# GpSimd zeroing of masked exponentials in twelve attention units, in place of mask products on TensorE

## The chip, the cores and the metric

The kernel runs on one core of a Trainium2 chip. The metric is the device time of one execution in microseconds. The kernel before was timed in three runs.

## What is computed

One decoder layer on 8 batches of 256 tokens, 256 features, in float32. It has three parts, each followed by a residual sum and a layer norm: self attention with 16 heads of 16 features, causal and with a window of 64 keys; cross attention to a context, 16 heads, causal, with ReLU on q, k and v; and a mixture of 8 experts, top 2, with capacity 160 in each of 2 groups. Cut to what matters here:

```python
# self attention
scores = einsum('bhid,bhjd->bhij', q, k) / sqrt(HD)
mask = (j <= i) & (j >= i - (W - 1))                 # W = 64
probs = softmax(where(mask, scores, -inf))
y = einsum('bhij,bhjd->bhid', probs, v) @ Wo.T + bo
# cross attention
scores = einsum('bqhd,bkhd->bhqk', relu(q), relu(k)) / sqrt(D)
probs = softmax(where(tril(ones), scores, NEG))
out = layer_norm(einsum('bhqk,bkhd->bqhd', probs, relu(v)) + q) * gamma + beta
# experts
dispatch, combine = top-2 routing with cumulative positions
y = combine . (relu((dispatch . x) @ wi) @ wo)
```

## The kernel before, in words

The attention work is cut into 16 units, `UNITS` (8 self "s", one for each batch, and 8 cross "c"). Units 0 to 3 are self, then they alternate: 4 is cross, 5 self, 6 cross, 7 self, 8 cross, 9 self, 10 cross, 11 self, and 12 to 15 are cross. Each unit has 12 jobs (`JOBS`), three for each of its four groups of four heads.

Each unit computes its scores twice on TensorE. The handler `N` computes them with queries on the partitions into one of two PSUM banks `nat`; VectorE takes the row maxima from them (`negm`). The maxima, split into three bf16 parts, are transposed (`MT`) and put as three extra rows under the queries. The handler `T_` then computes the transposed scores, keys on the partitions, minus these maxima, into one of two banks `byk`. ScalarE takes the exponential of a bank into `probs` (handler `T_` on ScalarE, line 769), which has two buffers, one for even and one for odd groups. Jobs 0 and 1 of a group hold the first 128 keys of two heads each, with 192 queries (self) or 256 (cross); job 2 holds the last 128 keys and queries of four heads. The handler `PV` (line 596) multiplies the exponentials by the values: 16 matmuls for a group. Ones beside the values give the sums of the softmax.

The mask comes in by TensorE: `bank_scores` starts a bank with a bf16 product of the identity and a mask tile that holds 0 and -3e38 (line 528), and then adds the score products of each head (line 532). A `byk` bank thus takes one mask product and two or four score products. The mask product is 384 columns wide for jobs 0 and 1 of a self unit, 256 for these of a cross unit, and 512 for job 2 of both.

The order of every engine's instructions is written out by hand. `in_order()` gives each piece of work a slot (a number of jobs since the start), sorts all pieces by slot into one list, `PLAN`, and each engine walks that list (`walk`) and issues the pieces it has a handler for, in that order, with blocking waits on semaphores. Unit k starts at `first_slot(k)`, 12k, plus 2 from unit 4 on; call it n0. Its `N` jobs have the slots n0 to n0+11, its `T` jobs n0+18 to n0+29 (a little earlier in units 0 to 2, by `SOONER`), its four `PV` n0+22.2+3g. ScalarE's exponential of a `T` job stands in the list at the slot of that job.

The pieces that GpSimd issues in the attention part are: `CK`, for a cross unit k at its n0-18, which splits the keys into bf16 parts. It waits for ScalarE's evacuations of that unit's key projection (`KC`, TensorE, at n0-19; ScalarE writes `parts_k` and then `fk`), and it is three operations of 128x512 (lines 1212 to 1214). `XB` (line 1221) and `XA` (line 1227), each one addition of 128x512. `VC` (line 1232), a ReLU in place on the values of a cross unit, at n0+10, which waits for VectorE's evacuation. `GS` (lines 1205 and 1252), the 16 indirect DMAs that send the tokens of the first group to the experts, from slot 166.1 on, 0.75 slots apart; some of them wait for the gates of the router or for earlier ones to land. And `ES`, the indirect DMAs of the expert outputs.

TensorE's `T_` job waits until the exponential of the job before the last has been read out of the bank; `PV` waits for the exponential of the third job of its group. The slots of `T` and `N` jobs around a `PV` run on while the exponential is computed.

After the attention the 16 expert passes run (`XT`, `H0`, `H1`, `H2`, `EY`, lines 655, 670, 684, 687), and then the last norm.

Of the kernel before, what the change touches and what calls it, by code (L numbers as in the profile page):

```python
# [8 lines left out]
ALU = mybir.AluOpType  # L9
# [3 lines left out]
P = 128  # L13
# [47 lines left out]

SOONER = {0: 6.05, 1: 4, 2: 2}
ROWS_BY_ACT = 3


CLOSING = {
# [23 lines left out]
def in_order():  # L90
# [7 lines left out]
    for k, (layer, b) in enumerate(UNITS):  # L98
        n0 = first_slot(k)
        sooner = SOONER.get(k, 0)  # L100
        if layer == "s":
            for later, earlier in X_BEFORE.items():
                if earlier == b:
                    add(n0 + (14.6 if b == 0 else 9.6), "LX", UNIT_OF["s", later])
            if b == 3:
                add(n0 + 9.7, "LC", UNIT_OF["c", 2])
            add(n0 + (14 if b == 0 else 8), "XL", k)
            for at, name in ((-12.4, "QS"), (-12.35, "SQ"), (-12.3, "KS"), (-12.2, "SK")) if b == 2 else ((-19, "QS"), (-18, "SQ"), (-17.5, "KS"), (-16.5, "SK")):
                add(n0 + at, name, k)
            for at, name in ((11.85 if b == 0 else 8.5, "VS"), (20, "XB"), (34 - sooner, "Y2"), (35 - sooner, "WO"), (36 - sooner, "R3"), (36.8 - sooner, "L3")):  # L110
                add(n0 + at, name, k)
        else:
            if b + TOK < B:
                add(n0 + 11.1, "LC", UNIT_OF["c", b + TOK])
            late = 2 if b == B - 1 else 0
            for at, name in ((-19, "KC"), (-18, "CK"), (late - 11.5, "XC"), (late - 10.2, "QC"), (late - 9.2, "SC"), (late - 6, "XA"), (10, "VC")):
                add(n0 + at, name, k)
            for at, name in CLOSING.get(k, ((n0 + 33.3, "FQ"), (n0 + 34.4, "R1"), (n0 + 35.2, "L1"), (n0 + 37, "R2"), (n0 + 37.7, "L2"),
                                            (n0 + 39.4, "XS"), (n0 + 39.5, "XR"), (n0 + 40.9, "RT"))):
                add(at, name, k)  # L120
        for j in range(JOBS):
            add(n0 + j, "N", k, j)
            add(t_slot(k, j), "T", k, j)
        add(n0 + (11.3 if k == 0 else 12), "MP", k)
        add(n0 + {0: 11.5, 1: 12.6, 2: 13.2}.get(k, 14) if k < last else 195.6, "MT", k)
        for g in range(G):
            add(n0 + 22.2 - sooner + 3 * g if k < last - 1 else t_slot(k, 3 * g + 2) + (1.1 if g < G - 1 else 0.5), "PV", k, g)
        add(n0 + 32.6 - sooner if k < last - 1 else (198.6, 206.9)[k - last + 1], "YA", k)
        add(n0 + 32.9 - sooner if k < last - 1 else (198.7, 207.0)[k - last + 1], "YB", k)
    for i, (at, _) in enumerate(LOADS):  # L130
# [58 lines left out]
def attention_and_experts(nc: bass.Bass, a, out):  # L189
    with ExitStack() as ctx:  # L190
# [124 lines left out]
        work_full = sems("work_full", WB); work_free = sems("work_free", WB)  # L315
        nat_full = sems("nat_full", 2); nat_free = sems("nat_free", 2)
        byk_full = sems("byk_full", 2); exp_ready = sem("exp_ready")
        pv_full = sem("pv_full"); yT_ready = sem("yT_ready")
        part0 = {side: sem(f"part0_{side}") for side in "qk"}
        split = {side: sem(f"split_{side}") for side in "qk"}  # L320
        stacked = {side: sems(f"stacked_{side}", PAIRS) for side in "qk"}
# [142 lines left out]
        def _(pe):  # L464
# [60 lines left out]
            def bank_scores(bank, mask, heads, w, at, emit_pair):  # L525
# [6 lines left out]
                    last = nc.tensor.matmul(bank[:, i * w:(i + 1) * w], lhsT, rhs, start=False, stop=(i == heads - 1), skip_group_check=True)  # L532
                return last

            def N(k, j, layer, b):
                q, ks = stack["q", k % PAIRS], stack["k", k % PAIRS]
                if j == 0:
                    if k == 0:
                        pe.wait_ge(masks_ready, 1)
                    pe.wait_ge(stacked["q"][k % PAIRS], SIDE * (k // PAIRS + 1))  # L540
                    pe.wait_ge(stacked["k"][k % PAIRS], SIDE * (k // PAIRS + 1))
                job = JOBS * k + j
                wait(pe, nat_free[job % 2], job // 2)
                g, i = divmod(j, 3)
                bank = nat[job % 2]
                if i == 0:
                    h0 = 4 * g
                    last = bank_scores(bank, mq0[layer], 4, P, 0, lambda h: (q[0:KR, h0 + h, 0:P], ks[0:KR, h0 + h, 0:P]))
                else:
                    h0, w = 4 * g + 2 * (i - 1), KEYS0[layer]  # L550
                    last = bank_scores(bank, mq1[layer], 2, w, w - mq1[layer].shape[2],
                                       lambda h: (q[0:KR, h0 + h, P:T], ks[0:KR, h0 + h, T - w:T]))
                last.then_inc(nat_full[job % 2], 1)
# [11 lines left out]
            def T_(k, j, layer, b):  # L565
                q, ks = stack["q", k % PAIRS], stack["k", k % PAIRS]
                if j == 0:
                    pe.wait_ge(m_rows[k % 2], 16 * MR * (k // 2 + 1))
                    if k < PAIRS:
                        pe.wait_ge(ones_in[k], 16)  # L570
                job = JOBS * k + j
                wait(pe, exp_ready, job - 1)
                g, i = divmod(j, 3)
                bank = byk[job % 2]
                if i < 2:
                    h0, w = 4 * g + 2 * i, KEYS0[layer]
                    last = bank_scores(bank, mk0[layer], 2, w, 0, lambda h: (ks[0:KR + MR, h0 + h, 0:P], q[0:KR + MR, h0 + h, 0:w]))
                else:
                    h0 = 4 * g
                    last = bank_scores(bank, mk1[layer], 4, P, 0, lambda h: (ks[0:KR + MR, h0 + h, P:T], q[0:KR + MR, h0 + h, P:T]))  # L580
                last.then_inc(byk_full[job % 2], 1)

            def PV(k, g, layer, b):
                pe.wait_ge(exp_ready, JOBS * k + 3 * g + 3)
                if g == 0:
                    if layer == "s":
                        emptied(pe, "VS", k)
                    else:
                        pe.wait_ge(v_ready, b + 1)
                if g % 2 == 0:  # L590
                    wait(pe, yT_ready, (G * k + g) // 2)
                o = (g % 2) * T
                for kt in range(QT):
                    for j in range(4):
                        cols, src = ((0, KEYS0[layer]), (0, KEYS0[layer])) if kt == 0 else ((P, T), (256, 384))
                        last = nc.tensor.matmul(pv[32 * j:32 * j + 32, o + cols[0]:o + cols[1]], vone[layer][:, b % 2, kt, 4 * g + j, :],  # L596
                                                probs[:, g % 2, j, src[0]:src[1]], start=(kt == 0), stop=(kt == QT - 1),
                                                skip_group_check=True)
                last.then_inc(pv_full, 1)
# [549 lines left out]
        def _(pool):  # L1149
# [53 lines left out]
            def put_gates(tile, tiles, k):  # L1203

                g_.tensor_copy(xres[:, tile:tile + tiles, GATE], gates[:, tile:tile + tiles, k]).then_inc(ids_ready, 1)

            def CK(k, n, layer, b):
                pool.wait_ge(part0["k"], k + 1)
                emptied(pool, "KC", k)
# [56 lines left out]
                                        out_offset=bass.IndirectOffsetOnAxis(ap=target[:, x % 2, 1:2], axis=0),  # L1266
                                        in_=ye[x % 2][:, 1, 0:ZW], in_offset=None, compute_op=ALU.add).then_inc(y_stored[x % 2], 16)

            walk({"CK": CK, "XB": XB, "XA": XA, "VC": VC, "GS": GS, "ES": ES})


def by_partition(a):
# [50 lines left out]
```

## Time and profile before

| | |
|---|---|
| median of 3 runs | 625.91 us (622.70 to 629.24) |
| the profiled execution, own time | 624.59 us |
| its span in the trace | 622.8 us |
| PE busy | 520.7 us, 84% of the span, 5092 matmuls |
| DVE busy | 338.3 us, 54% |
| ACT busy | 218.9 us, 35% |
| POOL busy | 146.8 us, 24%, 160 instructions |
| mean granted TensorE clock | 0.941 |

PE is TensorE's matmuls, PEld its weight loads, DVE VectorE, ACT ScalarE, POOL GpSimd. Busy times are of one profiled execution; 1.8 us of its own time lie outside the span. Matmuls are pipelined and their ends are modelled, so what a matmul costs is read from the distance of one start to the next. The attention part takes the span up to about 450 us, the experts follow to about 600 us.

### The profile page before, as it was taken

What the parts mean: (1) busy time and instruction counts of PE and PEld (TensorE: products, weight loads), DVE (VectorE), ACT (ScalarE), POOL (GpSimd) and SP (SyncE); (2) the same over time, 40 slices, a digit from 0 to 9 for tenths busy, and PEclk for the clock granted to TensorE, in tenths of its full rate; (3) what the DMA queues carried; (4) which work ended last, traced back from release to release, by engine and by line L of the source; (5) the groups of instructions that cost most, each with busy time, mean ns of one, the idle gap of its engine ahead of it and who ended that gap; (6) DMA issues with size and microseconds to landing.
All of it is one profiled execution on the core that took longest, in us unless ns stands there. A gap on an engine that the chain in (4) does not pass through costs nothing. (4 is left out here: it accounts for less than half of the span.)

```text
span 622.8 us, 12856 instructions
## 1 busy us (share of the span) xinstructions
PE 520.7 (84%) x5092; PEld 404.9 (65%) x5092; DVE 338.3 (54%) x952; ACT 218.9 (35%) x491; POOL 146.8 (24%) x160
## 2 busy tenths in 40 slices
PE   5179487959989989989999879799798999999960
PEld 4047265737666667767767656477587888888850
DVE  3547343746677877877677967684263202232114
ACT  2004125234445544544554625453521111232103
POOL 4000003002103004004104166000123755132330
PEclk9669779989999999999999989799999999999995
DMA  2999935693595585585449556345666634888214
GB/s 87 118 145 140 161 62 87 116 106 43 78 136 97 76 132 99 85 120 101 96 54 157 79 109 189 52 162 196 224 233 228 202 52 76 247 300 244 23 20 137
DMA packets 58840, 78.97 MB, mean 127 GB/s; under 512 B 9454, under 2 KB 52077, under 8 KB 55708
## 3 DMA queue, kind: packets, MB, share of 16 engines
q1 hardware_dynamic: 42236, 39.57, 41.1%
q10 hardware_dynamic: 10400, 33.29, 16.9%
q0 software_dynamic: 6144, 5.29, 5.3%
q8 instruction: 40, 0.66, 0.5%
q14 instruction: 20, 0.16, 0.1%
HBM read 40.32 MB, written 13.74 MB: 87 GB/s over the span
## 5 line engine op out<-in xcount | busy, mean ns | idle before, releaser
L956 DVE TENSOR_REDUCE negm<-nat 128x4 f32<-128x512 f32 (+2 forms) x192 | 120.0, 641 | 88.7 <-PE nat L532 86.5
L769 ACT ACTIVATE probs<-byk 128x512 f32<-128x512 f32 (+1 forms) x192 | 105.8, 562 | 116.0 <-PE byk L532 114.3
L532 PE MATMUL nat<-arena 96*128 96x128 bf16 (+2 forms) x512 | 73.8, 248 | 0.0
L532 PE MATMUL byk<-arena 99*128 99x128 bf16 (+2 forms) x512 | 71.8, 242 | 0.0
L532 PEld LDWEIGHTS nat<-arena 96*128 96x128 bf16 x512 | 46.9, 102 | 16.3 <-issue 3.2
L532 PEld LDWEIGHTS byk<-arena 99*128 99x128 bf16 x512 | 45.7, 99 | 18.1 <-issue 1.1
L1212 POOL TENSOR_TENSOR resk<-fk,parts_k 128x512 f32<-128x512 f32 x8 | 9.3, 1158 | 182.3 <-ACT fk L708 125.8
L528 PE MATMUL nat<-window_q,identb 128*128 128x384 bf16 (+1 forms) x96 | 35.9, 374 | 18.8 <-DMA arena<-parts_k 13.7
L528 PE MATMUL byk<-window_k,identb 128*128 128x384 bf16 (+1 forms) x96 | 34.2, 356 | 18.1 <-DMA arena<-mT 17.7
L670 PE MATMUL work<-yn_T,arena 128*128 128x160 f32 x256 | 40.1, 305 | 2.4 <-DVE r_s L1123 2.4
L670 PE MATMUL work<-woT,arena 128*128 128x160 f32 x256 | 39.8, 304 | 0.0
L528 PE MATMUL nat<-causal_q,identb 128*128 128x256 bf16 (+1 forms) x96 | 30.3, 315 | 10.2 <-DVE negm L956 5.6
L670 PEld LDWEIGHTS work<-yn_T,arena 128*128 128x128 f32 x256 | 35.6, 190 | 3.4 <-DVE r_s L1123 2.6
L478 PE MATMUL work<-xT,ws 128*128 128x256 f32 x112 | 30.9, 433 | 6.9 <-DMA xT<-in_x_T 6.9
L670 PEld LDWEIGHTS work<-woT,arena 128*128 128x128 f32 x256 | 35.5, 190 | 0.9
L1252 POOL DMA_INDIRECT expert_x<-xres,put x32 | 31.9, 995 | 12.6 <-issue 7.8
L528 PE MATMUL byk<-causal_k,identb 128*128 128x256 bf16 (+1 forms) x96 | 30.2, 315 | 0.8 <-ACT probs L769 0.7
L478 PEld LDWEIGHTS work<-xT,ws 128*128 128x128 f32 x112 | 23.9, 220 | 10.9 <-issue 5.8
L684 PE MATMUL work<-arena,ws 128*128 128x256 f32 x128 | 29.1, 380 | 0.7 <-ACT ws L859 0.7
L1221 POOL TENSOR_TENSOR xres<-xres,rows 128x512 f32<-128x512 f32 x8 | 10.2, 1269 | 82.1 <-DMA xres<-in_x 82.1
L684 PE MATMUL work<-arena,xT 128*128 128x256 f32 x128 | 29.1, 380 | 0.0
L596 PE MATMUL pv<-probs,v_c 128*32 128x128 f32 (+1 forms) x512 | 28.1, 338 | 0.7 <-ACT probs L769 0.7
(189 smaller groups left out, 895.3 us busy)
## 6 DMA issues: line engine op xcount, KB each, us to landing
arena<-parts_q SPq DMA_DIRECT2D x96, 128.0 KB, 5.1
arena<-parts_k SPq DMA_DIRECT2D x96, 128.0 KB, 5.4
arena<-in_ffn_wi ACTq DMA_DIRECT2D x12, 1024.0 KB, 5.5
arena<-in_ffn_wo ACTq DMA_DIRECT2D x12, 1024.0 KB, 8.4
expert_x<-ranked ACTq DMA_DIRECT2D x4, 650.0 KB, 4.9
v_s<-expert_x SPq DMA_DIRECT2D x20, 130.0 KB
xres<-in_x ACTq DMA_DIRECT2D x8, 256.0 KB, 5.5
token_y<-xres SPq DMA_DIRECT2D x8, 256.0 KB, 5.0
```

The source lines that it names most:

```text
L478: last = nc.tensor.matmul(bank[:, m * T:(m + 1) * T], w[:, c, m0 + m * P:m0 + (m + 1) * P], tokens[:, c, :], start=(c == 0), stop=(c == C ...
L528: nc.tensor.matmul(bank[:, 0:heads * w].rearrange("p (h t) -> p h t", t=w)[:, :, at:at + mw], identb[:, :], mask[:, :, :].broadcast_to([P, ...
L532: last = nc.tensor.matmul(bank[:, i * w:(i + 1) * w], lhsT, rhs, start=False, stop=(i == heads - 1), skip_group_check=True)
L596: last = nc.tensor.matmul(pv[32 * j:32 * j + 32, o + cols[0]:o + cols[1]], vone[layer][:, b % 2, kt, 4 * g + j, :], probs[:, g % 2, j, src ...
L670: mm = nc.tensor.matmul(bank[:, i * CAP:(i + 1) * CAP], wi[e % WSLOTS][:, c, f * P:(f + 1) * P], xeT[x % 2][:, c, :], start=(c == 0), stop ...
L684: nc.tensor.matmul(bank[:, 0:D], hT[x % 2][:, f, 0:P], wo[e % WSLOTS][:, f, :], start=(f == 0), stop=(f == FC - 1))
L769: nc.scalar.activation(dst, src, ACT.Exp, scale=0.25).then_inc(exp_ready, 1)
L956: V.tensor_reduce(dst, src, AX, ALU.max, negate=True).then_inc(nat_free[job % 2], 1)
L1212: link(g_.tensor_tensor(resk[:, :, :], fk[:, :, :], p[0], ALU.subtract))
L1221: g_.tensor_tensor(x_b, x_b, bo.unsqueeze(1).broadcast_to([P, QT, D]), ALU.add).then_inc(xb_ready, 1)
L1252: pool.indirect_dma_start(out=x_dram, out_offset=bass.IndirectOffsetOnAxis(ap=put[:, col:col + 1], axis=0), in_=xres[:, tile, :], in_offse ...
```

## The change

In the twelve units 2 to 13 (`ZEROED`: self units 2, 3, 5, 7, 9, 11 and cross units 4, 6, 8, 10, 12, 13) the transposed scores are computed without a mask product. After the exponentials GpSimd writes zeros over the entries outside the mask in `probs`, with `affine_select` in place. `Z0` follows the second exponential of a group and treats the first 128 keys: one select of 4x128 columns (causal), and in a self unit a second one of 4x128 columns (window), which waits for the first. `Z1` follows the third exponential: one select of 4x128 columns, and in a self unit a second one of 4x64. `PV` of these units waits for both, by the semaphore `zeroed`, and is moved 0.7 slots later in the list. The `N` scores and the units 0, 1, 14 and 15 keep their mask products.

```diff
+ZEROED = list(range(2, len(UNITS) - 2))
...
         for g in range(G):
-            add(n0 + 22.2 - sooner + 3 * g if k < last - 1 else t_slot(k, 3 * g + 2) + (1.1 if g < G - 1 else 0.5), "PV", k, g)
+            if k in ZEROED:
+                add(n0 + 20.1 + 3 * g, "Z0", k, g)
+                add(n0 + 21.3 + 3 * g, "Z1", k, g)
+            add(n0 + (22.9 if k in ZEROED else 22.2) - sooner + 3 * g if k < last - 1 else t_slot(k, 3 * g + 2) + (1.1 if g < G - 1 else 0.5), "PV", k, g)
...
+            def bare_scores(bank, heads, w, emit_pair):
+
+                for i in range(heads):
+                    lhsT, rhs = emit_pair(i)
+                    last = nc.tensor.matmul(bank[:, i * w:(i + 1) * w], lhsT, rhs, start=True, stop=True, skip_group_check=True)
+                return last
...
             def T_(k, j, layer, b):
...
-                if i < 2:
+                if k in ZEROED:
+                    if i < 2:
+                        h0 = 4 * g + 2 * i
+                        w = KEYS0[layer]
+                        last = bare_scores(bank, 2, w, lambda h: (ks[0:KR + MR, h0 + h, 0:P], q[0:KR + MR, h0 + h, 0:w]))
+                    else:
+                        h0 = 4 * g
+                        last = bare_scores(bank, 4, P, lambda h: (ks[0:KR + MR, h0 + h, P:T], q[0:KR + MR, h0 + h, P:T]))
+                elif i < 2:
...
             def PV(k, g, layer, b):
-                pe.wait_ge(exp_ready, JOBS * k + 3 * g + 3)
+                if k in ZEROED:
+                    pe.wait_ge(zeroed, 2 * (G * ZEROED.index(k) + g + 1))
+                else:
+                    pe.wait_ge(exp_ready, JOBS * k + 3 * g + 3)
...
+            def not_before(at, g):
+
+                kept = probs[:, g % 2, :, at:at + P]
+                return g_.affine_select(out=kept, in_=kept, compare_op=ALU.is_ge, fill=0.0, base=0, pattern=[[0, 4], [1, P]], channel_multiplier=-1)
+
+            def within_window(at, queries, g):
+
+                kept = probs[:, g % 2, :, at + WIN:at + queries]
+                return g_.affine_select(out=kept, in_=kept, compare_op=ALU.is_ge, fill=0.0, base=-1, pattern=[[0, 4], [-1, queries - WIN]],
+                                        channel_multiplier=1)
+
+            def Z0(k, g, layer, b):
+                pool.wait_ge(exp_ready, JOBS * k + 3 * g + 2)
+                last = not_before(0, g)
+                if layer == "s":
+                    link(last)
+                    last = within_window(0, KEYS0["s"], g)
+                last.then_inc(zeroed, 1)
+
+            def Z1(k, g, layer, b):
+                pool.wait_ge(exp_ready, JOBS * k + 3 * g + 3)
+                last = not_before(T, g)
+                if layer == "s":
+                    link(last)
+                    last = within_window(T, P, g)
+                last.then_inc(zeroed, 1)
...
-            walk({"CK": CK, "XB": XB, "XA": XA, "VC": VC, "GS": GS, "ES": ES})
+            walk({"Z0": Z0, "Z1": Z1, "CK": CK, "XB": XB, "XA": XA, "VC": VC, "GS": GS, "ES": ES})
```

## Rows read from the trace of the kernel before

**Rows 1.** Windows: us, busy (x instructions) of each engine, PEclk, DMA share, GB/s.

```profile
200.00:360.00 160.00, 146.49 (x1383) 108.22 (x1381) 124.62 (x343) 80.58 (x185) 32.01 (x28) 1.00 0.66 101
420.00:600.00 180.00, 171.78 (x1971) 147.90 (x1970) 54.13 (x213) 40.48 (x91) 63.05 (x49) 1.00 0.60 176
100.00:120.00 20.00, 15.37 (x123) 11.83 (x120) 9.38 (x21) 7.07 (x16) 1.27 (x1) 0.91 0.76 111
200.00:220.00 20.00, 18.60 (x165) 14.05 (x164) 16.90 (x43) 10.73 (x25) 3.06 (x2) 1.00 0.67 95
```

**Rows 2.** Waits of PE from 175 to 350 us: total us, times, longest.

```profile
PE nat L528 <- DVE negm L956: 5.5, 13, 1.0
```

**Rows 3.** Timeline of PE: start, us, instruction; two transposed jobs with their masks.

```profile
236.79 0.33 PE L528 MATMUL byk<-window_k,identb 128*128 128x384 bf16 x1
236.95 0.33 PE L532 MATMUL byk<-arena 99*128 99x192 bf16 x2
...
239.11 0.39 PE L528 MATMUL byk<-window_k,identb 128*128 128x512 bf16 x1
239.33 0.39 PE L532 MATMUL byk<-arena 99*128 99x128 bf16 x4
```

**Rows 4.** Groups of GpSimd by form: count, busy us, mean ns.

```profile
L1161 POOL TENSOR_SCALAR_AFFINE_SELECT window_k<-window_k 128x192 bf16<-128x192 bf16 x2 | 0.7, 343 | 0.0
L1161 POOL TENSOR_SCALAR_AFFINE_SELECT causal_k<-causal_k 128x128 bf16<-128x128 bf16 x1 | 0.3, 288 | 0.0
```

**Rows 5.** Timeline of GpSimd: the same addition (XA) at two places.

```profile
101.56 1.27 POOL L1227 TENSOR_TENSOR x<-x,rows 128x512 f32<-128x512 f32 x1 [2.69 <-PE work L472]
...
201.94 1.57 POOL L1227 TENSOR_TENSOR x<-x,rows 128x512 f32<-128x512 f32 x1 [0.37 <-PE work L472]
```

**Rows 6.** Timeline around the last PV of unit 6: KC, fk, PV, and CK.

```profile
235.06 1.89 PE L478 MATMUL work<-cT,wk_c 128*128 128x256 f32 x8
...
237.80 0.84 ACT L708 ACTIVATE fk<-work,bias 128x256 f32<-128x256 f32 x2
...
238.32 0.86 PE L596 MATMUL pv<-probs,v_c 128*32 128x256 f32 x16
...
238.77 1.16 POOL L1212 TENSOR_TENSOR resk<-fk,parts_k 128x512 f32<-128x512 f32 x1 [35.25 <-ACT fk L708]
...
240.69 1.15 POOL L1214 TENSOR_TENSOR parts_k<-resk,parts_k 128x512 bf16<-128x512 f32 x1
```

**Rows 7.** Timeline, PE and GpSimd: PVs of units 3 and 9, their GpSimd neighbours, a wait.

```profile
148.64 1.16 POOL L1214 TENSOR_TENSOR parts_k<-resk,parts_k 128x512 bf16<-128x512 f32 x1
...
150.39 0.75 PE L596 MATMUL pv<-probs,v_s 128*32 128x192 f32 x16
...
155.16 1.51 POOL L1232 TENSOR_SCALAR v_c<-v_c 128x512 f32<-128x512 f32 x1 [5.36 <-DVE v_c L936]
...
155.19 0.75 PE L596 MATMUL pv<-probs,v_s 128*32 128x192 f32 x16
...
307.04 0.75 PE L596 MATMUL pv<-probs,v_s 128*32 128x192 f32 x16
...
309.41 1.16 POOL L1214 TENSOR_TENSOR parts_k<-resk,parts_k 128x512 bf16<-128x512 f32 x1
...
360.33 0.66 PE L472 MATMUL work<-ident,ynat_s 128*128 128x128 f32 x4 [2.51 <-DVEq L1000]
```

**Rows 8.** Timeline, PE and GpSimd: unit 12, the indirect DMAs, and the wait after.

```profile
368.67 0.99 POOL L1252 DMA_INDIRECT expert_x<-xres,put  x1 [0.30 <-issue]
...
370.63 0.86 PE L596 MATMUL pv<-probs,v_c 128*32 128x256 f32 x16
...
394.14 0.61 PE L528 MATMUL nat<-causal_q,identb 128*128 128x512 bf16 x1 [4.46 <-DMA arena<-parts_q]
```

**Rows 9.** Windows around that wait, columns as in rows 1.

```profile
390.00:395.00 5.00, 0.86 (x6) 0.59 (x7) 3.37 (x15) 0.88 (x3) 0.68 (x1) 0.68 0.53 57
395.00:400.00 5.00, 5.00 (x44) 3.03 (x43) 3.37 (x9) 2.34 (x5) 0.00 (x0) 0.64 0.01 3
```

More of the change, by code:

```diff
@@ L317, in attention_and_experts @@
         byk_full = sems("byk_full", 2); exp_ready = sem("exp_ready")
-        pv_full = sem("pv_full"); yT_ready = sem("yT_ready")
+        pv_full = sem("pv_full"); zeroed = sem("zeroed"); yT_ready = sem("yT_ready")
         part0 = {side: sem(f"part0_{side}") for side in "qk"}
```

## The prediction

> **What bounds the kernel now.** I read the busy shares by stretch first, because the page's 84% for TensorE is an average over stages. From 200 to 360 us, the steady part of the attention, TensorE's matmuls are busy 146.5 of 160 us at full clock, VectorE 124.6 and GpSimd only 32.0; from 420 to 600 us, the experts, TensorE is busy 171.8 of 180 [rows 1]. The waits say how much of the rest is dependence: from 175 to 350 us TensorE waited 5.5 us in 13 pieces for VectorE's maxima, none over 1.0 us [rows 2]. The timeline shows its instructions start to start without holes. So TensorE's in-order stream is the bound: an instruction taken out of it is worth its whole start-to-start distance, and a new wait in it costs its whole length. What GpSimd does costs nothing by its amount. It costs where TensorE stands and waits for it. So the question is in which order GpSimd gets to each new piece.
>
> **The change, part by part.**
>
> *Mask products removed.* A mask of 384 columns starts 0.16 us before the score products behind it, one of 512 columns 0.22 us [rows 3]. The 256-column ones of cross units are two thirds of the first, 0.11 us (estimate). A self unit saves 8 x 0.165 + 4 x 0.22 = 2.2 us, a cross unit 8 x 0.11 + 4 x 0.22 = 1.76 us. Six of each: 13.2 + 10.6 = 23.8 us. The identity's weight load goes too, but loads overlap matmuls here, so I count nothing for it.
>
> Not all of this arrives. In units 12 and 13 about eight of the jobs stand ahead of a wait of 4.46 us for a DMA that does not hang on them [rows 8]; they are worth 8 x 0.15 = 1.2 us. Another 1.5 us lies between `KC` and a late `PV` (below), where TensorE only arrives earlier at a wait. 21.1 us remain.
>
> *Selects added.* No select of 4x128 float32 is in the trace. The nearest rows are the selects of 192 and 128 columns, 343 and 288 ns: 0.86 ns for each column more, so 512 columns take 288 + 384 x 0.86 = 0.62 us and 256 take 0.40 us [rows 4]. The lower bound is 0.29 us, if the width cost nothing; the upper is the one-input operation in place of 128x512 float32, 1.51 us [rows 7]. I take 0.62, since it is the same operation. With some 0.1 us for the semaphore, `Z1` costs 0.75 us in a cross unit and 1.15 us in a self unit, `Z0` 0.75 and 1.4. In all GpSimd gets 24 x 1.5 + 24 x 2.55 = 97 us more over some 300 us, where it is idle for four fifths: by amount this is hidden.
>
> *The new wait, ordinary case.* Before `PV` come, in TensorE's order, the `T` and `N` jobs of two more slots, so the exponentials are usually done 1 to 5 us before `PV` starts, and 0.7 slots more are given to it. Where nothing else is queued on GpSimd the selects fit, and I count nothing.
>
> *The new wait behind `CK`.* `Z1` of the last group of unit k has slot n0+30.3. `CK` of unit k+4 has slot n0+48-18 = n0+30 for k = 4, 6 and 8 and comes just ahead of it; the same holds in units 9, 10 and 11, with `CK` of 13, 14 and 15. `CK` is blocking: it waits until ScalarE has evacuated the key projection, which TensorE issued only two slots before that `PV`, and then runs three operations. In unit 6 `KC` starts at 235.06, `fk` is written from 237.80, `CK` runs from 238.77 to 240.69 + 1.15 = 241.84, and `PV` started at 238.32 [rows 6]. With `Z1` behind `CK`, `PV` can start at 241.84 + 0.75 = 242.6 at best: 4.2 us later. The sum is against the old clock of the trace, so what the removed masks gain between `KC` and `PV` is void, as said. Four cross units (4, 6, 8, 10) have this pattern: 16.8 us. In unit 9 it is 309.41 + 1.16 + 1.15 - 307.04 = 4.7 us [rows 7]. Unit 11 has it too, but 6 us later stands a wait of 2.51 us for VectorE [rows 7], which goes meanwhile: 0.8 us remain.
>
> *Unit 3.* `CK` of unit 6 (56.0) comes ahead of both `Z0` and `Z1` of the first group: 148.64 + 1.16 + 1.4 + 1.15 - 150.39 = 2.0 us. `VC` of unit 4 (60.0) comes ahead of `Z1` of the second: 155.16 + 1.51 + 1.15 - 155.19 = 2.6 us [rows 7], and as `VC` itself hangs on TensorE, this adds to the first. 4.6 us.
>
> *Units 12 and 13.* The selects share the queue with 16 indirect DMAs, 1.29 us apart [rows 8]. Up to `PV` of group 1 in unit 12 two or three of these and `VC` stand ahead, and `Z1` ends at some 372.4 us against 370.63: 1.8 us. Two more groups slip by 0.7 and 3 us, but these lie ahead of the 4.46 us wait [rows 8], which covers them. 1.8 us count.
>
> *What is late next.* VectorE catches up while TensorE stands, so part of the 5.5 us [rows 2] and of TensorE's short waits for the norms disappears: -3 us (bounds 0 and -7).
>
> *The clock.* After TensorE had stood 4.46 us the granted clock is 0.68 in the 5 us around that and 0.64 in the next 5 us, though TensorE is busy in all of these [rows 9]: that is the level of 1.2 GHz for part of both windows. From 395 to 400 this is 0.36 x 2 = 72% of 5 us at half speed, so 3.6 us of work in which half is lost, and with what is left of the window before about 2 us. The new pauses are 4.2 to 4.7 us long each. Five such pauses cost 5 x 2 = 10 us (bounds 0 and 15).
>
> The Trainium skill, "TensorE: Matmul & The Clock Gate", section "Part 1: The HAM clock gate", says that the default state is throttled and activity releases the throttle. The trace agrees at this one place. A price that went by the waits alone would be the sum below without the 10 us.
>
> *Sum.* Waits 16.8 + 4.7 + 0.8 + 4.6 + 1.8 = 28.7; clock +10; caught up -3; saved -21.1. That is +14.6 us on the profiled execution's own 624.6 us (span 622.8 and 1.8 outside): 639.2 us. The median of the runs lies 1.3 us above that execution, so I forecast 641 us.
>
> **The rivals.**
>
> *Pauses without a half clock, mostly absorbed.* The same waits, but TensorE's clock stays. For it: in the steady part short waits leave the clock at 1.00 [rows 1]. Against it: rows 9. 641 - 10 = 631 us.
>
> *The masks' time comes back.* The pauses behind `CK` are made up, because the engines behind TensorE (VectorE at 78% [rows 1]) have run empty and TensorE then runs through its next jobs without waits, and ScalarE evacuates `KC` earlier than I think. It would need 28.7 us of waits to shrink to some 8, with no clock loss: 625.9 + 8 - 21.1 = 613 us. For it speaks that there are more than 10 us of slack of VectorE in the steady part; against it that TensorE's own waits there are only 5.5 us [rows 2], so there is not much that a pause can take the place of.
>
> *Slow selects and a shared port.* The same addition took 1.27 us at 101.56 and 1.57 us at 201.94 [rows 5], in stretches where VectorE is busy 9.4 and 16.9 of 20 us [rows 1]. If a 512-column select takes 1.51 us and not 0.62, `Z1` grows by 0.9 to 1.2 us at five pauses (+5), the window of four indirect DMAs in unit 12 gets +3, and the groups of self units, with slack of 1 to 2 us and 5 us of selects in three slots of 1.9 us, wait 3 to 4 us in each of six units (+20): 641 + 28 = 669 us. The Trainium skill, "GPSIMD Engine Reference", section "8. Key points", says that GpSimd shares its SBUF interfaces with VectorE, with contention for some VectorE instructions, and calls it the wrong choice for ordinary elementwise work. This speaks against the change in the same direction; rows 5 agree with a quarter more, which on 0.62 us would be nothing that matters.
>
> **How the numbers follow.** Forecast 0.55, no half clock 0.16, masks' time comes back 0.14, slow selects 0.15. The unknown costs of the likeliest (clock 0 to 15, catching up 0 to -7, select 0.29 to 1.51) span 628 to 655 us by themselves. The range 616 to 660 us takes in the second rival, part of the third and part of the fourth, and leaves out the rest, some 0.2. Within 1% (619.7 to 632.2) is about what a measurement of this kernel can tell from no change; faster than that is the third rival less a little, 0.12; within it lie half of the second and the edges of the others, 0.13; slower 0.75.
>
> **What would show it.** In the profile after: 144 fewer matmuls at the mask line of `byk`, and selects of about 0.62 us. `PV` of the last group in units 4, 6, 8, 9 and 10 with a wait of 4 to 5 us put down to GpSimd, starting about 0.1 us after `Z1`, and `Z1` right behind line 1214. The granted clock under 1.00 in the 5 us after each of these, where it is 1.00 now. TensorE's busy time down by about 30 us by the trace's count, less what the half clock adds. Waits for VectorE below 5.5 us in the steady part. The forecast is wrong if GpSimd's selects reach `PV` without a wait at these places, if the pauses are there but the clock stays at 1.00, or if selects take over 1 us.

## The result, and the profile after

The changed kernel takes 684.85 us, median of 4 runs (682.88 to 686.97), against 624.77 us (622.70 to 629.24) for the kernel before: 1.095 times as long, 95% interval 1.0915 to 1.0987. I had forecast 641 us, with 660 us as the upper end. The direction is right, the size is not: 60 us lost where the forecast had 15 (641 against the 625.91 us it started from).

The same windows as in [rows 1], of the kernel after; the experts are now 60 us later:

```profile
200.00:360.00 160.00, 126.01 (x1077) 93.22 (x1070) 98.92 (x240) 63.21 (x144) 66.85 (x90) 0.88 0.53 83
480.00:660.00 180.00, 170.04 (x1938) 146.70 (x1936) 53.34 (x212) 40.26 (x91) 62.37 (x49) 0.99 0.60 175
```

The experts did not change. In the attention TensorE gets through 1077 matmuls in 160 us where it was 1383 (part of the fall is the mask products that are gone, 12 for each changed unit), it is idle for 34 us of the 160, and its granted clock, 1.00 before, is 0.88. The selects themselves are as I priced them (GpSimd's groups by form, in the kernel after):

```profile
L1232 POOL TENSOR_SCALAR_AFFINE_SELECT probs<-probs 128x512 f32<-128x512 f32 x96 | 65.4, 683 | 128.1 <-ACT probs L791 128.1
L1237 POOL TENSOR_SCALAR_AFFINE_SELECT probs<-probs 128x512 f32<-128x512 f32 x24 | 15.9, 662 | 1.6
L1237 POOL TENSOR_SCALAR_AFFINE_SELECT probs<-probs 128x256 f32<-128x256 f32 x24 | 11.7, 490 | 1.6
```

The mean of 0.68 us for 512 columns stands against 0.62 forecast; most of the single ones take 0.64; the narrow ones of 4x64 columns take 0.49 against 0.40. And here is unit 6, the place of [rows 6], in the kernel after (timeline of PE, ACT and POOL):

```profile
257.30 1.89 PE L482 MATMUL work<-cT,wk_c 128*128 128x256 f32 x8
...
260.04 0.84 ACT L730 ACTIVATE fk<-work,bias 128x256 f32<-128x256 f32 x2
...
261.01 1.15 POOL L1261 TENSOR_TENSOR resk<-fk,parts_k 128x512 f32<-128x512 f32 x1 [5.40 <-ACT parts_k L730]
262.24 0.61 POOL L1262 CAST parts_k<-resk 128x512 bf16<-128x512 f32 x1
262.93 1.15 POOL L1263 TENSOR_TENSOR parts_k<-resk,parts_k 128x512 bf16<-128x512 f32 x1
264.03 0.64 POOL L1232 TENSOR_SCALAR_AFFINE_SELECT probs<-probs 128x512 f32<-128x512 f32 x1
...
264.73 1.51 PE L618 MATMUL pv<-probs,v_c 128*32 128x256 f32 x16 [4.43 <-POOL probs L1232]
```

This is the forecast chain link by link: KC, fk, the three operations of CK, one select, and PV starting 0.06 us after it. The wait is 4.43 us; I had said 4 to 5 us. The same row stands at units 4, 8 and 10 with 4.4 us and at unit 9 with 4.8 us. Note also that the PV's 16 matmuls take 1.51 us there in place of 0.86: they run at the lower clock (the granted clock is 0.50 from 265 to 270 us).

What I had not forecast is in the rest of TensorE's waits (whole span, kernel after):

```profile
PE pv L618 <- POOL probs L1232: 24.5, 9, 4.4
PE nat L532 <- DVE negm L978: 19.7, 26, 2.5
PE pv L618 <- POOL probs L1237: 12.9, 4, 4.8
...
PE work L572 <- DVE mp L989: 8.3, 9, 2.4
...
PE work L476 <- DVE xres L1056: 7.1, 7, 1.8
```

37.4 us for selects, where the sum had 28.7. And TensorE waits more for VectorE, not less: 19.7 us for the maxima, in 26 pieces, where the kernel before has, over its whole span,

```profile
PE nat L528 <- DVE negm L956: 10.4, 21, 1.5
```

I had expected VectorE to catch up in the pauses. Two questions follow. Why did the missing mask products give nothing back? And what slowed VectorE's side, when its own work is unchanged?

### The profile page after: what moved, and what is told of

Its sections match the earlier page's. It is cut to its first block and busy times, and to the rows that moved or that the text cites. A ratio compares the mean times of both kernels' runs of the same rounds, so it can differ in the third digit from the quotient of the medians.

```text
span 684.8 us, 12712 instructions
## 1 busy us (share of the span) xinstructions
PE 533.2 (78%) x4948; PEld 413.8 (60%) x4948; DVE 350.2 (51%) x952; ACT 219.1 (32%) x491; POOL 237.1 (35%) x304
## 5 line engine op out<-in xcount | busy, mean ns | idle before, releaser
L1232 POOL TENSOR_SCALAR_AFFINE_SELECT probs<-probs 128x512 f32<-128x512 f32 x96 | 65.4, 683 | 128.1 <-ACT probs L791 128.1
L536 PE MATMUL nat<-arena 96*128 96x128 bf16 (+2 forms) x512 | 78.9, 260 | 0.0
L543 PE MATMUL byk<-arena 99*128 99x128 bf16 (+2 forms) x384 | 59.3, 263 | 6.0 <-DMA arena<-mT 4.7
L618 PE MATMUL pv<-probs,v_c 128*32 128x128 f32 (+1 forms) x512 | 32.6, 381 | 25.2 <-POOL probs L1232 24.5
L543 PEld LDWEIGHTS byk<-arena 99*128 99x128 bf16 x384 | 31.9, 106 | 22.6 <-issue 10.5
L532 PE MATMUL nat<-causal_q,identb 128*128 128x256 bf16 (+1 forms) x96 | 34.2, 356 | 12.2 <-DVE negm L978 12.1
L618 PEld LDWEIGHTS pv<-probs,v_c 128*32 128x32 f32 x512 | 14.8, 121 | 40.0 <-POOL probs L1232 27.3
L618 PE MATMUL pv<-probs,v_s 128*32 128x128 f32 (+1 forms) x512 | 27.1, 335 | 12.9 <-POOL probs L1237 12.9
L800 ACT ACTIVATE yT<-pv 128x512 f32<-128x512 f32 x32 | 19.2, 601 | 53.2 <-PE pv L618 51.2
L1312 POOL DMA_INDIRECT token_y<-ynat_s,target x8 | 12.4, 1547 | 55.9 <-DVE ynat_s L1145 44.6
L1270 POOL TENSOR_TENSOR xres<-xres,rows 128x512 f32<-128x512 f32 x8 | 10.2, 1269 | 62.1 <-DMA xres<-in_x 62.1
```

The lines of the kernel that those rows point to most:

```text
L532: nc.tensor.matmul(bank[:, 0:heads * w].rearrange("p (h t) -> p h t", t=w)[:, :, at:at + mw], identb[:, :], mask[:, :, :].broadcast_to([P, ...
L800: nc.scalar.activation(yT[:, g - 1:g + 1, :], two(pv), ACT.Copy).then_inc(yT_ready, 1)
L1232: return g_.affine_select(out=kept, in_=kept, compare_op=ALU.is_ge, fill=0.0, base=0, pattern=[[0, 4], [1, P]], channel_multiplier=-1)
```

## The experiments

The experiments ran in three series, each with the kernel before beside them: at 624.3 us (the first three experiments below and the selects as mere load), at 624.9 us (the moved PV, the masks out with PV unmoved, the filler in place of the masks, and masks and selects both) and at 624.6 us (the shorter maxima and the filler in the pauses). The ratios are against the kernel before of the same series.

### CK behind the selects

```diff
-            for at, name in ((-19, "KC"), (-18, "CK"), ...
+            for at, name in ((-19, "KC"), (-18, "CK"), (-16.6 if k == 6 else -17.6, "CP"), ... (10, "VC"), (10.5, "VP")):
...
-            walk({"Z0": Z0, "Z1": Z1, "CK": CK, "XB": XB, "XA": XA, "VC": VC, ...
+            walk({"Z0": Z0, "Z1": Z1, "CP": CK, "XB": XB, "XA": XA, "VP": VC, ...
```

VC, the other piece that stood ahead of selects, goes half a slot later too.

> The changed kernel with one edit: GpSimd takes CK of a later unit just behind the selects of the earlier one (slot n0-17.6 in place of n0-18, for unit 6 n0-16.6) and VC half a slot later. Theory A (order and clock: TensorE stands behind CK, and each pause drops its clock): in the changed kernel TensorE waited 37.4 us for selects; some 25 us of this goes, and with it some 20 us that the half clock costs, so 640 us, with the time at half clock down from 150 to about 100 us. Theory B (port: the selects slow VectorE, and the time is lost in its chains): the waits move to VectorE and the time stays over 670 us.

653.72 us, ratio 1.044 (1.037 to 1.051). Its waits of PE:

```profile
PE nat L532 <- DVE negm L978: 17.6, 21, 2.5
...
PE pv L618 <- POOL probs L1237: 4.9, 4, 1.2
...
PE pv L618 <- POOL probs L1232: 3.5, 3, 1.9
```

The waits for selects fall from 37.4 to 8.4 us and the time by 31.1 us. The forecast's terms that this edit can take away were 16.8 + 4.7 + 0.8 + 4.6 of waits, 10 of clock and -3: 33.9 us. So the waits that the forecast put down to GpSimd's order are right in place and in size: 26.9 us in the sum, 29.0 measured. The rest of the two totals agrees by luck: the forecast has 7 us more for clock and catching up, the runs 2. And 29 us of loss remain that this order does not mend, between the numbers of theories A and B.

### The pauses alone

```diff
+LATE = {4: 8, 6: 10, 8: 12, 9: 13, 10: 14, 11: 15}
...
                 pe.wait_ge(exp_ready, JOBS * k + 3 * g + 3)
+                if g == 3 and k in LATE:
+                    pe.wait_ge(split["k"], LATE[k] + 1)
```

> The kernel before with its mask products and without selects, but the last PV of units 4, 6, 8, 9, 10 and 11 waits until CK of the later unit is done. Six pauses of TensorE of 3.5 us (2.1 in unit 11), nothing else. Theory A: 18 to 20 us of pauses and 2 to 3 us of clock for each, so 625 + 19 + 13 = 657 us. Theory B, or pauses that are made up: under 640 us.

655.17 us, ratio 1.045 (1.037 to 1.053): 30.9 us lost. The profile puts down 20.1 us to the new wait (waits of PE, whole span):

```profile
PE pv L599 <- POOL parts_k L1217: 20.1, 6, 3.6
```

A pause is not made up for afterwards. In this kernel it costs its own length and half as much again, 10.8 us over six pauses, 1.8 us each. From 200 to 350 us the granted clock is 0.95, where the kernel before has 1.00. That the total is nearly the 31.1 us of the experiment above is a coincidence: there 29.0 us of waits went, those of unit 3 among them, here 20.1 us came. A us of wait is worth 1.07 us there and 1.54 us here, and no run shows why. The waits for the maxima are 10.0 us in this kernel, 10.4 in the kernel before: pauses alone let VectorE catch up by almost nothing.

### Masks out, no selects

```diff
-                if k in ZEROED:
-                    pe.wait_ge(zeroed, 2 * (G * ZEROED.index(k) + g + 1))
-                else:
-                    pe.wait_ge(exp_ready, JOBS * k + 3 * g + 3)
+                pe.wait_ge(exp_ready, JOBS * k + 3 * g + 3)
...
-            walk({"Z0": Z0, "Z1": Z1, "CK": CK, ...
+            walk({"CK": CK, ...
```

> The changed kernel without any select and with PV waiting for the exponentials alone, as before; the mask is left out of the twelve units' exponentials. What the removed mask products are worth when nothing is paid for them. If TensorE's stream is the bound, as I forecast: 21 us under the kernel before, 604 us. If VectorE or the DMA chains bound it as much: 615 us or more.

632.08 us, ratio 1.011 (1.007 to 1.016). With 144 mask products less and no select in their place (only PV still stands 0.7 slots later), the kernel is slower than before. This is the step that I had taken as safest. The window and the waits of PE from 200 to 350 us, the kernel before (window, waits), then this one (window, waits):

```profile
200.00:350.00 150.00, 139.85 (x1321) 103.28 (x1320) 115.76 (x294) 75.83 (x175) 28.89 (x24) 1.00 0.64 99
```

```profile
PE nat L528 <- DVE negm L956: 4.9, 12, 1.0
PE work L472 <- DVE xres L1034: 2.6, 4, 0.8
PE work L472 <- DVEq L1000: 1.5, 3, 0.5
```

```profile
200.00:350.00 150.00, 132.04 (x1193) 97.55 (x1191) 110.63 (x282) 72.88 (x170) 26.76 (x23) 0.94 0.65 97
```

```profile
PE nat L532 <- DVE negm L975: 8.7, 13, 1.3
PE work L476 <- DVE xres L1053: 3.2, 4, 0.8
PE work L476 <- DVEq L1019: 1.8, 3, 0.6
```

TensorE's busy time falls by 7.8 us, but VectorE's work done in the window falls too, from 115.8 to 110.6 us: the kernel as a whole got on more slowly. TensorE waits longer for VectorE, and its clock is down to 0.94, though none of its recorded waits there, for whatever engine, is longer than 1.3 us. Two causes are mixed in it, the clock and VectorE, and a third, the moved PV. Five kernels took them apart.

### The moved PV alone, and masks out with PV unmoved

The first is the kernel before with PV 0.7 slots later, the second the one above with `22.2` in place of `(22.9 if k in ZEROED else 22.2)`.

> The kernel before with one edit: PV of units 2 to 13 stands 0.7 slots later in the list. Masks stay, no selects. Asked: was it this move, and not the missing masks, that brought the kernel without selects to 632 us in place of 604? If the move is to blame: 635 us or more. If it is harmless: 622 to 628 us.

628.51 us, ratio 1.0057 (1.0024 to 1.0091): just over the band I had called harmless, and clear of no change. The 0.7 slots that were to give GpSimd time cost 3.6 us themselves.

> The kernel without mask products and without selects (the mask is left out in twelve units), PV at its old slot. If TensorE's stream is the bound and only the moved PV spoilt it: 604 us. If TensorE then meets VectorE and a lower clock whatever PV does: 622 to 634 us.

624.38 us, ratio 0.998 (0.994 to 1.001). With PV where it was, taking out 24 us of TensorE's work changes nothing that can be told from zero. So the loss in the kernel above, 7.7 us against this one, is the moved PV's, twice what it costs with the masks in place, and the missing masks are worth 0.5 us in place of 21. From 200 to 350 us the clock is 0.97 here and 0.94 in the kernel above; why the later PV costs clock without the masks, no run shows.

### Filler in place of the masks

```diff
             def XR(k, n, layer, b):
+                fill("XR", k, 3)
                 pe.wait_ge(x2_ready, b + 1)
...
             def Y2(k, n, layer, b):
+                fill("Y2", k, 2)
                 pe.wait_ge(ynat_ready, b + 1)
...
+                fill("RT", k, 1)
                 emptied(pe, "XR", k)
```

`fill` waits until the work bank is free and writes products of the identity and a mask tile into it, which the real work then overwrites.

> The kernel without mask products and selects, with filler products of 512 bf16 columns whose result nobody reads, issued ahead of three waits in each of the units 2 to 13: three before XR's, two before Y2's, one before RT's (some 0.65, 0.43 and 0.22 us at full clock, where TensorE stood 0.8, 0.6 and 0.2 us). The mask is left out as there. If the missing masks cost clock because TensorE is less active: the clock is back at 1.00 from 200 to 350 us and the time falls by 8 us to some 624 us, though TensorE has more to do. If VectorE alone is the bound: no change in the time, 632 us.

625.08 us, ratio 0.999 (0.995 to 1.002), 7.0 us under the same kernel without filler (632.08, with PV late as here). The window from 200 to 350 us:

```profile
200.00:350.00 150.00, 135.37 (x1277) 98.42 (x1277) 117.29 (x304) 75.83 (x175) 28.82 (x24) 1.00 0.67 101
```

The clock is back at 1.00. Products whose result nobody reads made the kernel faster, because TensorE is active where it had stood for fractions of a microsecond. This answers what the mask products also did: in stretches of short jobs with short waits they were part of the activity that held the 2.4 GHz level. But PV is late in this kernel too, so its fair partner is the kernel with masks and late PV, 628.51 us: with the clock back, the missing masks are worth 3.4 us and not 21, so the clock is only one of the two reasons. The filler with PV unmoved was not run.

### Half as much to read for the maxima

```diff
-                V.tensor_reduce(dst, src, AX, ALU.max, negate=True).then_inc(nat_free[job % 2], 1)
+                V.tensor_reduce(dst, src[:, :, ::2], AX, ALU.max, negate=True).then_inc(nat_free[job % 2], 1)
```

once without masks and selects, once in the kernel before.

> The kernel without mask products and selects, PV at its old slot (624.4 us), and VectorE's row maxima taken over every second key, so that each reduction reads half the columns; the mask is left out of twelve units' exponentials and the maxima are not the exact ones. If VectorE took over as the bound when the masks went, the 21 us come now: 604 us or less. If the DMA chains or the norms' dependences bind: 615 us or more.

612.19 us, ratio 0.978 (0.973 to 0.983).

> The kernel before with only the row maxima over every second key, masks in place; the maxima are not the exact ones. If TensorE's stream alone bounds the kernel before, as my forecast had it: 620 us or more. If VectorE and TensorE bound it together: 612 us or less.

621.57 us, ratio 0.9946 (0.9922 to 0.9970). With the mask products in place the shorter maxima save 3.1 us: there TensorE's stream is nearly the whole bound, as I had read it. Without the mask products they save 12.2 us. Seen the other way, taking the masks out is worth 0.5 us with the full maxima and 9.4 us with the short ones. VectorE is the second reason: the time its maxima take begins to count as soon as TensorE has less to do. But 612 us is in neither of my two expected bands; even with the short maxima, less than half of the 21 us arrives. What holds the rest was not tried further; the waits of PE from 200 to 350 us in the kernel with short maxima and no masks point to other chains of VectorE, the scaling of the self attention's output (the first row, one wait of it 2.7 us) and the norms (the last), but no run shows it:

```profile
PE work L476 <- DVEq L1019: 4.6, 4, 2.7
PE nat L532 <- DVE negm L975: 4.0, 8, 0.8
PE work L476 <- DVE xres L1053: 2.4, 4, 0.7
```

### The selects as mere load

The kernel before with its masks, plus all 144 selects on a scratch tile, in the same places of GpSimd's list, behind the same exponentials; nobody waits for them.

```diff
+        spare_probs = sb("spare_probs", [P, 4, 192])
...
+                kept = spare_probs[:, :, 0:P]
+                return g_.affine_select(out=kept, in_=kept, ...
...
+                kept = spare_probs[:, :, WIN:queries]
```

> The kernel before with its mask products, and in addition all selects, in the same order on GpSimd and after the same exponentials, but on a scratch tile, and nobody waits for them. GpSimd's load and the port alone. Theory A: VectorE's busy time grows by 10 to 12 us as in the changed kernel, the time by 5 us at most (630 us). Theory B: 20 us or more (645 us and above).

640.26 us, ratio 1.021 (1.013 to 1.029): 16.0 us for work that nobody waits for, between the two theories' numbers and nearer to B. VectorE by form, in the kernel before and then in this one:

```profile
L956 DVE TENSOR_REDUCE negm<-nat 128x4 f32<-128x512 f32 x64 | 43.9, 687 | 34.2 <-PE nat L532 33.0
L1019 DVE SCALAR_TENSOR_TENSOR r_c<-r_c,mv_c,rows 128x256 f32<-128x256 f32 x16 | 7.0, 482 | 0.4
L908 DVE TENSOR_TENSOR parts_k<-res_sk,parts_k 128x512 bf16<-128x512 f32 x8 | 5.5, 692 | 0.3
L981 DVE TENSOR_TENSOR rstd_c<-rstd_c,newton 128x2 f32<-128x2 f32 x16 | 2.6, 161 | 0.5
L980 DVE TENSOR_SCALAR newton<-newton 128x2 f32<-128x2 f32 x24 | 4.4, 181 | 0.8
```

```profile
L961 DVE TENSOR_REDUCE negm<-nat 128x4 f32<-128x512 f32 x64 | 43.9, 686 | 32.5 <-PE nat L537 31.3
L1024 DVE SCALAR_TENSOR_TENSOR r_c<-r_c,mv_c,rows 128x256 f32<-128x256 f32 x16 | 9.0, 603 | 0.4
L913 DVE TENSOR_TENSOR parts_k<-res_sk,parts_k 128x512 bf16<-128x512 f32 x8 | 6.8, 848 | 0.3
L986 DVE TENSOR_TENSOR rstd_c<-rstd_c,newton 128x2 f32<-128x2 f32 x16 | 4.4, 278 | 0.5
L985 DVE TENSOR_SCALAR newton<-newton 128x2 f32<-128x2 f32 x24 | 5.9, 247 | 0.8
```

The reductions, which read PSUM, keep their 0.69 us. Some of the operations on SBUF grow: two of the big ones by 120 to 160 ns, one of two columns from 161 to 278 ns. Not all do: the product at line 1027 has a mean of 737 ns before and 713 ns here. The growth is where the two engines run at the same time. Of the sixteen two-column products of `rstd_c` (line 986 in this kernel), eleven have no select beside them and take 0.16 us each, as before; the five that start within a select take 0.47 to 0.55 us. The two-column operations stand in the norm chains, one behind the other, and TensorE waits at their ends: its waits for the norms' results (`xres`) grow from 4.9 to 6.4 us over the whole span, and with those for the maxima, for their split and for the scaled outputs of self attention, from 25.3 to 34.0 us. That places 9 of the 16 us; where the rest goes was not worked out. VectorE's busy time rises from 338.3 to 352.0 us, in the changed kernel to 350.2.

The rival is that the selects delay GpSimd's other pieces in its queue. TensorE, VectorE and ScalarE are not recorded waiting for a GpSimd operation in this kernel. The DMA queue does wait for CK's parts of the keys, but in the kernel before as well (76.0 us there, 77.0 here), and TensorE's waits for the DMAs of those parts do not grow (13.7 and 12.5 us). So this delay shows in no wait.

One place in the changed kernel shows the two engines beside each other (timeline, POOL, then DVE):

```profile
276.13 0.64 POOL L1232 TENSOR_SCALAR_AFFINE_SELECT probs<-probs 128x512 f32<-128x512 f32 x1
276.84 0.64 POOL L1237 TENSOR_SCALAR_AFFINE_SELECT probs<-probs 128x512 f32<-128x512 f32 x1
277.43 0.82 POOL L1232 TENSOR_SCALAR_AFFINE_SELECT probs<-probs 128x512 f32<-128x512 f32 x1
...
276.29 0.48 DVE L1003 TENSOR_TENSOR rstd_c<-rstd_c,newton 128x2 f32<-128x2 f32 x1
276.81 1.71 DVE L1049 SCALAR_TENSOR_TENSOR r_c<-r_c,rstd_c,x 128x256 f32<-128x256 f32 x2
```

The two-column product takes 0.48 us there, the two products behind it 1.71 us together, and the third select 0.82 us in place of 0.64: both engines are slower than alone. The Trainium skill, "GPSIMD Engine Reference", section "8. Key points", says that GpSimd shares its SBUF interfaces with VectorE and contends with its two-port and two-input operations. The trace agrees for the two-input ones, and the reductions from PSUM, which are untouched, fit too. An operation with one input of two columns grows as well, from 181 to 247 ns; whether it ran in a two-port mode, no run here shows.

### Masks and selects both

The kernel with CK behind the selects, with `T_` as in the kernel before, so that the mask is applied twice.

> The kernel with the selects and CK behind them (653.7 us), with the mask products put back as well, so that the mask is applied twice. If mask products are worth their 24 us on TensorE: 675 us. If they run in time that VectorE sets and hold the clock up: 650 to 658 us.

646.16 us, ratio 1.035 (1.030 to 1.041): 7.6 us faster than with the mask products out, with 24 us more of work on TensorE. The two intervals (1.037 to 1.051 for the other) overlap by a little, though no run of the one is within the other's (644.9 to 649.6 against 651.2 to 654.6 us), so that it is faster is likely and not settled; that the products are not worth 24 us is settled. Its clock from 200 to 350 us is 1.00, the other's 0.95. Waits for selects remain, 8.2 us (waits of PE, whole span):

```profile
PE pv L610 <- POOL probs L1224: 4.6, 3, 3.2
PE pv L610 <- POOL probs L1229: 3.6, 4, 0.9
```

### Filler in the pauses

```diff
+                if g == 3 and k in (4, 6, 8, 9, 10):
+                    fill(pv[:, T:2 * T], 34, T)
                 if k in ZEROED:
                     pe.wait_ge(zeroed, 2 * (G * ZEROED.index(k) + g + 1))
```

> The changed kernel, with 34 filler products of 256 bf16 columns (3.6 us) in the unread half of the pv bank, issued where TensorE waits behind CK, in units 4, 6, 8, 9 and 10. The waits stay, TensorE is active in them. The clock's share of these five pauses: 2 to 3 us each, so 670 to 675 us in place of 685. If the clock did not matter: 685 us or a little more.

679.97 us, ratio 1.086 (1.081 to 1.091), against 1.095 for the changed kernel: 5.8 us less by the ratios, 1.2 us for each pause. The clock has a share in the pauses, about half of what I had put on it here. The window from 200 to 350 us:

```profile
200.00:350.00 150.00, 130.35 (x1166) 98.09 (x1164) 96.75 (x237) 60.43 (x137) 64.97 (x90) 0.93 0.57 89
```

The granted clock rises from 0.88 to 0.93 only. Behind the filler it holds: the PV of units 4, 6, 8 and 10 takes 0.86 us again, in place of 1.51. But it is 0.61 and 0.70 in the two windows of 5 us from 270 us on, where the last waits are of 0.3 to 1.1 us. So a good part of the half clock in the changed kernel belongs to the many short waits and not to the five long ones.

The second filler kernel is the kernel before:

```diff
                     if k == 15:
+                        wait(pe, nat_free[0], JOBS * k // 2)
+                        fill(nat[0], 18)
...
                 if j == 0:
+                    if k in (1, 3):
+                        wait(pe, exp_ready, JOBS * k - 1)
+                        fill(byk[0], 40 if k == 1 else 20)
                     pe.wait_ge(m_rows[k % 2], 16 * MR * (k // 2 + 1))
```

and 8 ahead of `Y2` of unit 11.

> The kernel before, with filler products (512 bf16 columns, result unread) in a free bank ahead of its four long waits: 40 ahead of the first transposed job of unit 1 (TensorE stood 10.5 us), 20 ahead of that of unit 3 (4.85), 8 ahead of Y2 of unit 11 (2.51), 18 ahead of the first N job of unit 15 (4.46). Nothing else changes. If a pause costs clock because TensorE is inactive, the half clock behind these four goes: 2.1 + 1.75 + 1.7 + 2.2 = 7.8 us, 617 us. If it comes by itself, or the work behind the pauses is not set by TensorE: 625 us.

620.98 us, ratio 0.9925 (0.9901 to 0.9949). In [rows 9] the wait ended at 394.1 us; here the filler runs from 383.1 to 387.2 and the wait ends at 387.6. The windows behind it, in this kernel:

```profile
390.00:395.00 5.00, 5.00 (x60) 3.88 (x57) 3.08 (x8) 2.96 (x7) 0.00 (x0) 1.00 0.14 34
395.00:400.00 5.00, 4.46 (x51) 3.24 (x50) 3.02 (x6) 2.75 (x5) 0.00 (x0) 1.00 0.87 263
```

The half clock is gone there (from 375 to 390 us it is 1.00 as well), and the mean granted clock of the profiled execution goes from 0.941 to 0.968. 3.7 us come of it, half of the 7.8 that I had worked out, and this is a version that beats both kernels, by less than 1% of the kernel before but clear of no change.

## Why the prediction was wrong

The loss of 60 us, laid out along kernels that ran. The last two steps are one edit each, the first is several; the kernels come from different series, in which the kernel before stood within 0.6 us:

| step | from | to | us |
|---|---|---|---|
| selects added, CK behind them, PV moved, masks kept | 624.9 | 646.2 | +21.3 |
| mask products taken out | 646.2 | 653.7 | +7.6 |
| CK and VC put ahead of selects | 653.7 | 684.9 | +31.1 |

*Mask products removed: wrong, and the largest error.* The sum had -21.1 us; the runs show -0.5 alone (+3.6 with the late PV, 632.08 against 628.51) and +7.6 beside the selects. The start-to-start distances were read rightly, and TensorE's matmuls did shrink, from 520.7 to 506.5 us busy with PV unmoved. What failed is the step before, "an instruction taken out of it is worth its whole start-to-start distance". I took the short waits of 5.5 us [rows 2] as proof that VectorE was far from being the bound, though its 124.6 of 160 us [rows 1] stood beside it. That row was also not all: I wrote that TensorE's instructions stand start to start without holes, but from 200 to 350 us it is idle for 10.2 us of 150, and 9.6 of these are waits for VectorE, of which the maxima are 4.9. Short waits here meant that VectorE is just fast enough for TensorE's pace, not that it has room for a faster one. And I took a busy share of TensorE as something with only a price; it also held the clock.

*Selects hidden by amount: wrong.* "What GpSimd does costs nothing by its amount" failed: 16.0 us as mere load. I had the sign in the rival of slow selects, from the addition of 1.27 and 1.57 us [rows 5], but looked only at what sharing does to the selects (0.68 for 0.62 us) and not at what it does to VectorE. So 0.64 us of select can cost another engine's critical chain 0.3 us or more. The first step in the table has 5.3 us more than that. The moved PV (3.6 us alone) and 8.2 us of waits for selects that the mended order keeps lie in it; as they sum to more, they must partly cover each other, which no run takes apart.

*The wait behind CK, unit 3: right.* Place, order of events and length were as written, 4.43 us for 4.2, 4.8 for 4.7, and 2.1 and 2.7 for 2.0 and 2.6 in unit 3. With clock and catching up the order was 33.9 us by the forecast and 31.1 us by the runs; of this total the waits are right, and the clock and the catching up, 7 us in the sum and 2 in the runs, had errors that partly cancel.

*Units 11, 12 and 13: about right.* TensorE waits 3.3 us at unit 11, where I counted 0.8 after a wait of 2.51 us behind it; that wait is down to 0.7 us. At groups 1 to 3 of unit 12 it waits 2.07, 0.32 and 3.25 us for 1.8, 0.7 and 3, and the DMA wait of 4.46 us that was to cover the last two is gone, as I had it. These waits that cover others are most of the difference between 37.4 and 28.7 us. No run isolates them.

*Catching up, -3 us: wrong.* With pauses alone the waits for the maxima stay (10.0 us for 10.4). In the changed kernel they rise to 19.7: they are 15.5 us with the selects as mere load and 16.9 us with the masks out, so both parts of the change feed them.

*The clock: mechanism right, size off.* Pauses alone cost 1.8 us each beyond their length; filler in them gave back 1.2 us each in the changed kernel and 0.9 each in the kernel before. I had 2. But the clock also fell where no long pause is, and that was not in the sum at all. The half clock is also why TensorE's busy time, which I expected to fall by about 30 us, rose from 520.7 to 533.2 us.

*The rivals.* None was it as priced. Pauses without a half clock are refuted by the clock of 0.88; that the masks' time comes back is refuted too, as pauses are not made up. "Slow selects and a shared port" was nearest in number and had the right cause at the wrong end, and its 669 us would still have been short.

## What to carry to other kernels

Before counting the work taken off the busiest engine as gained, look at the next busy one: short waits for it can mean that the two run in step, and a kernel with its work cut short (here the maxima over half the keys) tells for one run how much is there. Work put on an idle engine can be paid for by another one that works beside it, here 16 us, so try it first as mere load, unwaited. And where pieces of a hand-ordered queue block, place the new piece by what stands ahead of it: 0.4 to 1.4 slots of order were worth 31 us here, and the waits that made most of it were readable from the trace.

## What the runs showed of the hardware that I had not expected

TensorE's granted clock was 0.94 from 200 to 350 us in a kernel whose recorded waits there were all 1.3 us or shorter, and 1.00 again when filler products were put into its short waits, with 7.0 us gained. VectorE's operations of two columns on SBUF grew from 161 to 278 ns in the mean beside GpSimd's selects (0.16 us without a select at the same time, 0.47 to 0.55 us with one); its reductions from PSUM did not change (687 and 686 ns).
